# Attention over 32 heads: units of two heads with both halves of the queries in the four column tiles, sums in two banks by turns, and 24 trial items ahead instead of 40

## What is computed

```
xn = layer_norm(x, norm_w, norm_b)
q = (xn @ q_w + q_b).reshape(Bx, Tx, H, -1)
k = (xn @ k_w + k_b).reshape(Bx, Tx, H, -1)
att = jnp.einsum('bnhl,bmhl->bnmh', q, k)
att = att + (1.0 - mask) * -1000000.0
att = jax.nn.softmax(att, axis=2)
v = ((xn @ v_w + v_b) * src_mask[:, :, None]).reshape(Bx, Tx, H, -1)
y = jnp.einsum('bnmh,bmhl->bnhl', att, v).reshape(Bx, Tx, Dx)
h = layer_norm(y, sb_norm_w, sb_norm_b) * (1.0 + scale) + shift
return x + silu(h) @ out_w + out_b
```

## Time and profile before

| what | us |
|---|---|
| median of the runs | 1933.98 |
| the profiled execution | 1932.16 |
| its span | 1930.0 |
| in it: projections and trial items ahead of the main loop | 1433.9 to 1525.9 |
| main loop of the attention, up to the last score | 1525.9 to 1904.9 |
| tail of sequence 1 | 1904.9 to 1930.0 |

### The profile page before, as it was taken

How to read it: one execution, slowest core, us unless ns; L and a number is a source line. 1 busy time by engine, 2 the same in 40 slices (tenths; PEclk the granted TensorE clock), 3 DMA queues, 4 the chain that set the end, 5 groups by cost and what they waited for, 6 DMA issues and landing times.

```text
span 1930.0 us, 32286 instructions
## 1 busy us (share of the span) xinstructions
PE 1828.1 (95%) x12120; PEld 1309.9 (68%) x12120; DVE 1599.9 (83%) x2101; ACT 1424.0 (74%) x2661; POOL 1090.9 (57%) x615
## 2 busy tenths in 40 slices
PE   6989899998999999999999999999997999999997
PEld 3664899848997599969985899699963323332323
DVE  5565899668998699889995999799977999999742
ACT  3426899368993899799965999799954377777775
POOL 3031799537994499959970899599935300003000
PEclk9989899999999999999999999999998799999999
DMA  5023111121121111101110112111101111111000
GB/s 203 1 86 100 61 56 60 39 68 37 58 59 38 50 58 56 50 29 57 56 39 9 39 60 56 33 65 59 56 9 36 39 41 38 36 36 36 17 24 22
DMA packets 57545, 95.15 MB, mean 49 GB/s; under 512 B 14951, under 2 KB 23559, under 8 KB 55982
## 3 DMA queue, kind: packets, MB, share of 16 engines
q1 hardware_dynamic: 55854, 88.90, 15.1%
q0 software_dynamic: 1536, 4.20, 0.7%
HBM read 73.55 MB, written 6.91 MB: 42 GB/s over the span
## 4 chain that ended last, share of the span: by engine, by line
PE 43%; POOL 24%; issue 12%; ACT 11%; DVE 8%; DMA 1%; SPq 1%; DVEq 0%; ACTq 0%; POOLq 0%
POOL A L1020 23%; PE PS L256 7%; PE PS L1604 6%; PE PS L1557 6%; PE PS L1764 5%; PE PS L265 3%; PE PS L862 3%; ACT A L928 3%; DVE A L1570 2%; PE PS L837 2%; PE PS L441 2%; PE PS L843 2%; ACT A L905 1%; ACT A L912 1%; PE PS L243 1%
## 5 line engine op out<-in xcount | busy, mean ns | idle before, releaser
L1020 POOL TENSOR_TENSOR A<-A 128x1024 f32<-128x1024 f32 x384 | 896.4, 2401 | 39.2 <-DVE A L997 25.8
L928 ACT ACTIVATE A<-A,negA 128x512 f32<-128x512 f32 x768 | 546.9, 715 | 34.0 <-DVE A L997 24.1
L997 DVE TENSOR_TENSOR_SCAN A<-A,PS 128x512 f32<-128x512 f32 x384 | 434.8, 1200 | 27.5 <-PE PS L843 16.2
L997 DVE TENSOR_TENSOR_SCAN A<-A,small,PS 128x512 f32<-128x512 f32 x384 | 451.2, 1258 | 5.3 <-ACT A L928 5.3
L862 PE MATMUL PS<-ident,A 128*128 128x128 f32 x3072 | 408.5, 276 | 23.5 <-ACT A L736 13.4
L837 PE MATMUL PS<-A 128*128 128x128 f32 x3072 | 392.7, 277 | 1.5 <-ACT A L912 1.2
L862 PEld LDWEIGHTS PS<-ident,A 128*128 128x128 f32 x3072 | 351.7, 142 | 33.6 <-ACT A L736 15.8
L837 PEld LDWEIGHTS PS<-A 128*128 128x128 f32 x3072 | 368.9, 192 | 5.5 <-DVE A L997 2.8
L1570 DVE TENSOR_REDUCE A<-PS 128x1 f32<-128x512 f32 x512 | 319.5, 681 | 40.5 <-PE PS L1557 38.9
L1801 ACT ACTIVATE A<-PS 128x512 f32<-128x512 f32 x512 | 267.5, 602 | 102.2 <-PE PS L1764 101.9
L905 ACT ACTIVATE A<-A,small 128x512 f32<-128x512 f32 x320 | 228.4, 714 | 7.2 <-PE PS L843 7.1
(11 more groups left out here) (194 smaller groups left out, 1826.7 us busy)
## 6 DMA issues: line engine op xcount, KB each, us to landing
A<-scrc SPq DMA_DIRECT2D x192, 256.0 KB, 3.1
A<-A SPq DMA_DIRECT2D x360, 32.0 KB
scr<-A SPq DMA_DIRECT2D x4, 1024.0 KB, 4.8
W<-in_wa SPq DMA_DIRECT2D x2, 1536.0 KB, 9.8
X<-in_x SPq DMA_DIRECT2D x4, 512.0 KB, 5.6
scr<-W SPq DMA_DIRECT2D x128, 1.5 KB
out<-X SPq DMA_DIRECT2D x4, 512.0 KB, 2.9
W<-in_w SPq DMA_DIRECT2D x1, 1984.0 KB, 7.6
```

The costliest lines, as they stand in the source:

```text
L928: e.activation(A_B[i % 4], r.DT[:, dt, ci * 512:(ci + 1) * 512], ACT.Exp, scale=negA[:, r.n, dt * 16 + s:dt * 16 + s + 1]).then_inc(*decay ...
L997: e.tensor_tensor_scan(h, a, u, init, ALU.mult, ALU.add).then_inc(*scanned.up((q, i)))
L1020: e.tensor_tensor(h, h, CB[k % 2].unsqueeze(1).broadcast_to([128, 2, 512]), ALU.mult).then_inc(*weighed.up((q, pair)))
```

## The change

1. HQ is 2: a unit is two heads, there are 16 units, and a step is what a half-step was (128 steps). The four column tiles hold two heads by two halves of the queries, so the value matmuls stand as one group of four per step (`weigh_t`).
2. The sums of unit u go to bank u % 2. A unit's sums wait only for the copy of unit u-2. The whole bank is copied by ScalarE in one instruction (`normalise_s`); VectorE's copy is gone. Four transposes and one reciprocal per unit, one key block later than before (mt = 2).
3. PX has four buffers, by mt % 4, of two heads each. An exponent waits for the value matmuls four steps back; the first four steps each wait for one of the split parts.
4. LEAD is 24. The item of a step is LEAD + 16u + 2mt + j.
5. On SP, stacks from 11 on stand one by one, after the key blocks 1 and 5 of the units from u = 1 on; stack 11 comes after step (1, 1), stack 12 after (1, 5). Stacks 3 to 10 hang on the trial items as before.
6. The tail of sequence 0 and its statistics are placed by the count of pairs of steps, at the same count of half-steps as before.

```diff
-        H, HQ, LEAD = 16, 4, 40
+        H, HQ, LEAD = 16, 2, 24
-        PX = [[area(16384 + 1024 * (4 * p + j), S) for j in range(HQ)] for p in range(2)]
+        PX = [[area(16384 + 1024 * (HQ * p + j), S) for j in range(HQ)] for p in range(4)]
...
-        def weigh_t(e, w, u, mt, c):
+        def weigh_t(e, w, u, mt):
             b, g = units[u]
-            for j in range(HQ):
-                h, tile = HQ * g + j, b * TB + mt
-                if mt == 0 and u:
-                    w.wait_ge(*(dve.at(("upper", u - 1)) if c else act.at(("lower", u - 1))))
-                w.wait_ge(*act.at(("weights", u, mt, j, c)))
...
+            if mt == 0 and u >= 2:
+                w.wait_ge(*act.at(("taken", u - 2)))
+            for c in range(2):
+                for j in range(HQ):
+                    h, tile, q = HQ * g + j, b * TB + mt, HQ * c + j
+                    w.wait_ge(*act.at(("weights", u, mt, j, c)))
+                    w.wait_ge(*act.at(("v3", tile)))
+                    t = e.matmul(PV[32 * q:32 * q + 32, u % 2, :], V[:, tile * 272 + 17 * h:tile * 272 + 17 * h + 32],
+                                 PX[mt % 4][j][:, c * 512:(c + 1) * 512], start=mt == 0, stop=mt == TB - 1, tile_position=(0, 32 * q),
+                                 skip_group_check=True)
...
             for u, mt, last in steps():
                 for j in range(HQ):
-                    ahead_sp(e, w, LEAD + 32 * u + 4 * mt + j)
-                if mt == TB - 1:
-                    for j in range(HQ):
-                        stack_sp(e, w, HQ * u + SLOTS + j)
+                    ahead_sp(e, w, LEAD + 16 * u + 2 * mt + j)
+                if u and mt in (1, 5):
+                    stack_sp(e, w, HQ * (u - 1) + SLOTS + mt // 4)
...
-                    if last and j % 2:
-                        weigh_t(e, w, *last, j // 2)
-                if u and mt == 1:
+                if last:
+                    weigh_t(e, w, *last)
+                if u and mt == 2:
                     normalise_t(e, w, u - 1)
...
-            for n in range(2):
-                for h in range(2):
-                    w.wait_ge(*pool.at(("parts", 1, h, n)))
             for u, mt, last in steps():
+                step = TB * u + mt
+                if step < 4:
+                    w.wait_ge(*pool.at(("parts", 1, step % 2, step // 2)))
+                else:
+                    w.wait_ge(*pe.at(("weighed", (step - 4) // TB, (step - 4) % TB)))
```

More of the change, by code:

```diff
@@ L1407, in program @@
         NM = area(35008, 2, 2 * TB)
-        RC = area(35040, TB, HQ)
+        RC = area(35040, 2, 16)
         MR = area(24576, 128)[0:16, :]
@@ L1609, in normalise_t @@
-        def normalise_t(e, w, u):
[L1610 to L1615, removed]
-        def normalise_s(e, w, u):
[L1618 to L1627, removed]
+            if mt == 0 and u >= 2:
[8 more added lines that the diff above has]
+                                 skip_group_check=True)
@@ new lines, in weigh_t @@
+            t.then_inc(*pe.up(("weighed", u, mt)))
+        def normalise_t(e, w, u):
+            o = take(w, ("turned", u), first)
+            w.wait_ge(*act.at(("taken", u)))
+            for q in range(4):
+                t = e.transpose(o[:, q * 128:(q + 1) * 128], PVs[:, u % 2 * 512 + q * 128:u % 2 * 512 + (q + 1) * 128], ident[:, :])
+            t.then_inc(*pe.up(("turned", u)))
+        def normalise_s(e, w, u):
+            w.wait_ge(*pe.at(("weighed", u, TB - 1)))
+            if u >= 2:
+                w.wait_ge(*pe.at(("turned", u - 2)))
+            e.activation(PVs[:, u % 2 * 512:(u % 2 + 1) * 512], PV[:, u % 2, :], ACT.Copy).then_inc(*act.up(("taken", u)))
@@ L1631, in normalise_v @@
             y = Yt[:, b * TB:(b + 1) * TB, HQ * 16 * g:HQ * 16 * (g + 1)].rearrange("p q (j e) -> p q j e", j=HQ)
-            for c in range(2):
[L1633 to L1641, removed]
+            f = bank(("turned", u)).rearrange("p (t e) -> p t e", e=32)
+            f5 = bank(("turned", u)).rearrange("p (q c j e) -> p q c j e", c=2, j=HQ, e=32)
+            r = RC[:, u % 2, :]
+            r4 = r.rearrange("p (q c j) -> p q c j", c=2, j=HQ)
+            w.wait_ge(*pe.at(("turned", u)))
+            if u >= 2:
+                w.wait_ge(*dve.at(("y3", u - 2)))
+            e.reciprocal(r, f[:, :, 16]).then_inc(*dve.up())
+            w.wait_ge(*dve.now())
+            for c in range(2):
+                e.tensor_tensor(y[:, 4 * c:4 * c + 4], f5[:, :, c, :, 0:16], r4[:, :, c, :].unsqueeze(3).broadcast_to([128, 4, HQ, 16]), ALU.mult).then_inc(*dve.up(("y3", u)))
+            banks.give(("turned", u), dve.now())
         LAST = (range(TB, TB + 4), range(TB + 4, NT))
@@ L1681, in tail_p, with pairs_of_steps @@
                     norm_p(e, w, ("lny3", half[0]), half)
+        def pairs_of_steps(u, mt):
+            return divmod(TB * u + mt, 2)[0] if mt % 2 else None
         def tail_due(u, mt):
-            return 3 * (u - 5) + (1, 4, 7).index(mt) if u in (5, 6) and mt in (1, 4, 7) else None
+            n = pairs_of_steps(u, mt)
+            return (41, 44, 47, 49, 52, 55).index(n) if n in (41, 44, 47, 49, 52, 55) else None
         def layer3_sp(e, w):
@@ L1729, in layer3_p @@
                 for j in range(HQ):
-                    ahead_p(e, w, LEAD + 32 * u + 4 * mt + j)
-                if u == 4 and mt == 7:
+                    ahead_p(e, w, LEAD + 16 * u + 2 * mt + j)
+                if pairs_of_steps(u, mt) == 39:
                     tail_p(e, w, 0, 0)
@@ L1760, in layer3_t @@
                     for c in range(2):
-                        ahead_t(e, w, LEAD + 32 * u + 4 * mt + j, (c,))
+                        ahead_t(e, w, LEAD + 16 * u + 2 * mt + j, (c,))
                         o = take(w, ("score", u, mt, j, c), scores)
@@ L1771, in layer3_t @@
                     tail_t(e, w, 0, tail_due(u, mt), scores if tail_due(u, mt) < 2 else first)
-            for c in range(2):
-                weigh_t(e, w, len(units) - 1, TB - 1, c)
+            weigh_t(e, w, len(units) - 1, TB - 1)
             normalise_t(e, w, len(units) - 1)
@@ L1787, in layer3_s @@
                 front_s(e, w, job)
-            for n in range(2):
-                for h in range(2):
-                    w.wait_ge(*pool.at(("parts", 1, h, n)))
             for u, mt, last in steps():
+                step = TB * u + mt
[3 more added lines that the diff above has]
+                    w.wait_ge(*pe.at(("weighed", (step - 4) // TB, (step - 4) % TB)))
                 for j in range(HQ):
-                    if j == 3 and u and mt == 0:
+                    if j == 1 and u and mt == 1:
                         normalise_s(e, w, u - 1)
-                    step = 8 * u + mt
                     for c in range(2):
@@ L1798, in layer3_s @@
                         w.wait_ge(*pe.at(key))
-                        if step >= 2:
-                            w.wait_ge(*pe.at(("weighed", (step - 2) // 8, (step - 2) % 8, c)))
-                        e.activation(PX[mt % 2][j][:, c * 512:(c + 1) * 512], bank(key), ACT.Exp).then_inc(*act.up(("weights", u, mt, j, c)))
+                        e.activation(PX[mt % 4][j][:, c * 512:(c + 1) * 512], bank(key), ACT.Exp).then_inc(*act.up(("weights", u, mt, j, c)))
                         banks.give(key, act.now())
@@ L1827, in layer3_v @@
                     for c in range(2):
[L1828 to L1831, removed]
+                        ahead_v(e, w, LEAD + 16 * u + 2 * mt + j, (c,))
+                if u and mt == 2:
                     normalise_v(e, w, u - 1)
[L1833 to L1836, removed]
+                n = pairs_of_steps(u, mt)
+                if n in range(35, 39):
+                    w.wait_ge(*dve.at(("y3", len(units) // 2 - 1)))
+                    stats_v(e, ("lny3", 0), lambda i: Yt[:, i, :], (2 * (n - 35), 2 * (n - 35) + 1))
+                if n == 39:
                     moments_v(e, w, ("lny3", 0), range(TB))
@@ L1839, in layer3_v @@
                     tail_v(e, w, 0, tail_due(u, mt))
-            take_upper_v(e, w, len(units) - 1)
             normalise_v(e, w, len(units) - 1)
```

## The result

The changed kernel takes 1940.74 us (median of 6 runs, 1939.49 to 1942.1), the kernel before 1934.07 in the same comparison. The ratio is 1.0037, with a 95% interval of 1.0024 to 1.0050: slower by 6.7 us. The forecast was 1936.3, in a range of 1928 to 1944, with 0.37 on slower by more than 0.2%. The range held and the mechanism was in the main the one forecast (SP's order of issue takes back what LEAD 24 gives); "same" had the larger chance, and the result is just beyond it.

What follows compares the result with a forecast made beforehand. Bound taken: VectorE ahead of the main loop, TensorE in it, with SP's queue to watch. Terms: -17.7 + 2.1 + 15.0 + 2.9 = +2.3 us on 1932.16, 1934.5; as median 1936.3, range 1928 to 1944.

Steps and rivals of the forecast that it cites:

- same: Outcome class for the whole kernel: time within 0.2% (3.9 us), 1930.1 to 1937.9; chance 0.48.
- Rows 7: Rows of head 7 in SP's list: issued after eight stacks and five rows, done at 1594.1, landed at 1595.4.
- the wait for head 5: TensorE at step (2, 0): rows of head 5 land at 1556.9, wanted at 1554.8; wait of 2.1 us.
- the wait for head 7: TensorE's score of head 7: rows land at 1595.4, wanted at 1580.4; wait of 15.0 us.
- the clock: TensorE after the 15 us wait: 5.9 us at half clock, costing +2.9 us, bounds 0 and 4.1.
- LEAD and the start: Main loop's start: 32 trial matmuls leave the VectorE-bound run, -19.1 us; first three half-steps faster, -1.9 us.
- Turns: Turning the sums inside the loop: fifteen at 0.69 us instead of seven at 1.37, +0.7 us; +3.9 at 0.9 each.
- no further wait follows: SP after the rows of head 7: 21.8 us per unit of two heads against TensorE's 23.5, so no later wait.
- The rows did not come in time: Rival on SP: rows of head 7 reached before 1579, only -17.7 us left, 1916.3 us; chance 0.12.
- SP paces the loop: Rival in the main loop: a stack and rows pair on SP takes 12.2 us, total 1950; chance 0.07.
- The high end of the range: Upper bound on total time: +3.0 for slower stacks, +1.2 for the clock, +3.2 for turns, giving 1943.7 us.

Runs made afterwards that it cites:

- e1: Changed kernel with stacks from 11 on put into SP's list one and a half units later; 1923.84 us, ratio 0.9950.
- e6: Changed kernel with the five DMAs of each head's rows issued from GpSimd instead of SP; 1921.68 us, ratio 0.9941.
- e2: Changed kernel with LEAD 40 instead of 24, all else as in the change; 1936.1 us, ratio 1.0015.
- e5: Changed kernel with the edits of e1 and e3 together; 1918.77 us, ratio 0.9917 to the kernel before.
- e7: Kernel of e5 with one transpose instead of four in each turn inside the loop, part of the result left out; 1914.67 us, ratio 0.9911.
- e3: Changed kernel with GpSimd's block of eight normalisations of sequence 0 spread as two per step over four steps; 1936.78 us, ratio 1.0017.
- e4: Changed kernel with only stack 13 moved on SP, behind the rows of head 7; 1940.8 us, ratio 1.0030.

## Why the prediction was right, point by point

- **SP.** The order was read from the code and the durations from the trace, and both held. Rows 7 were forecast at SP until 1594.1 and ended at 1594.2, the wait for head 5 was forecast at 2.1 and was 1.6, the wait for head 7 15.0 and was 14.0; the clock was forecast at 2.9 and was about 2.3. The experiments e1 and e6 show that the order on SP is the cause, and e1 that nothing else had to change. The two waits together came out 1.9 us smaller than forecast, clock included, which hides a part of the misses below.
- **LEAD and the start.** -21.0 forecast, -20.7 measured, and 17.3 against 17.4 (21.0 - 3.6) between e2 and e5.
- **Turns.** The step that failed in size. The prediction took half of 1.37 and named 0.9 as the bound; it measured 0.82, because 0.37 of a turn does not depend on the transposes (e7) and stands in each of the fifteen. That is 2.0 us.
- **The third wait.** The step that was missing. The prediction says "no further wait follows", from SP's own rate of 21.8 us per unit against 23.5. It had looked for what delays SP only in SP's list. The rows also hang on GpSimd, where a block of 9.7 us of another stage stands in the list; the kernel before had so much lead that no score waited behind the block. This is 4.2 us by value groups, and e3 shows it (4.0 by the medians).
- **The rivals.** The rows did not come in time, as the queue said; the Trainium skill's sentence that a sequencer's time to initiate a DMA is usually small relative to the DMA itself ("DMA: Bandwidth & Descriptors", section "Issuing engines are not separate DMA queues") does not fit this kernel, where 13 DMAs of a stack occupy SP for 8.0 to 9.2 us and a small read is there 1.35 us after its issue. That SP paces the loop did not happen either: from 1635 on it has gaps in each unit (the first from 1634.79 to 1635.34). The price of that rival was added up a little short: units 3 to 11 are nine, and 9 x 0.9 is 8.1, not about 7.
- **The chances.** With the two misses of +2.0 and +4.2 the time moved from inside "same" to just above it. The high end of the range, 1943.7, had the turns in it but nothing for a delay from GpSimd.

## What to carry to other kernels

When a lead is shortened, every in-order queue between producer and consumer has to be written out with its durations up to the deadline, SP among them, and each other stage's block in those queues counts as well. Issue time of DMAs is work like any other: place the transfers that nobody needs yet behind those that somebody waits for. If one wait is cured, ask where the queue's debt comes due next.

## What was not expected of the hardware

Short standstills of TensorE cost more than their length. In the kernel after, 1.64 us left the granted clock at 1.00, and 2.59 us was followed by half clock; in e3 a wait of 1.71 us already was, and in e4 one of 1.68. The windows of e3 behind its wait of 1.71 us, and of the kernel after behind the 2.59 us:

```profile
1558.00:1560.00 2.00, 1.93 (x11) 0.38 (x11) 0.69 (x1) 1.09 (x2) 0.13 (x1) 0.82 0.22 53
1560.00:1562.00 2.00, 2.00 (x9) 0.63 (x6) 0.92 (x2) 0.60 (x1) 0.00 (x0) 0.50 0.22 51
```

```profile
1790.00:1792.00 2.00, 1.82 (x11) 0.38 (x11) 0.69 (x1) 1.08 (x2) 0.00 (x0) 0.80 0.25 56
1792.00:1794.00 2.00, 2.00 (x8) 0.58 (x5) 0.69 (x1) 0.34 (x1) 0.00 (x0) 0.50 0.14 30
```

Nor is the length of the wait what decides. In e5 a score waits 1.30 us for ScalarE, and the clock falls; in e2 the same score waits the same 1.30 us, with the same 0.97 us of idle time 4 us ahead of it, and the clock stays at 1.00. First e5, then e2:

```profile
1781.39 0.39 PE L1765 MATMUL PS<-A 102*128 102x512 bf16 x1 [1.30 <-ACT A L1800]
...
1782.00:1784.00 2.00, 2.00 (x11) 0.57 (x4) 0.00 (x0) 0.81 (x2) 0.00 (x0) 0.50 0.22 52
```

```profile
1798.71 0.39 PE L1763 MATMUL PS<-A 102*128 102x512 bf16 x1 [1.30 <-ACT A L1798]
...
1799.00:1801.00 2.00, 2.00 (x16) 0.88 (x16) 0.26 (x1) 1.12 (x3) 0.00 (x0) 1.00 0.07 13
```

Where the clock fell in the loop, the half clock took another 1.3 us (e5) to 2.7 us (e4, behind the wait of 4.65), measured by value groups. What else decides whether it falls is open.

The profiled executions also differ by up to 4.6 us in when the last layer begins (the mask's read starts between 1431.77 in e2 and 1436.33 in e5), though all these kernels are the same up to there. Single executions of this kernel can't tell apart edits of 2 us; the stretch between value groups can.
